# Row stage of a small language-model tower: layer norms, transposes and expert gates in other operations

## The reference

```python
h = tok_ref(x, token_W, pe)
h = h + attn_ref(layernorm(h), ...)       # softmax(qk + bias) * scale @ v, proj, then layernorm(out) * ln2_g + ln2_b
h = h + ffn_ref(layernorm(h), ...)

# ffn_ref
gate_logits = x_flat @ Wg + bg + bias
topk_vals, topk_idx = top_k(gate_logits, 2)
topk_w = softmax(topk_vals, axis=-1)
combine = (one_hot(topk_idx, 8) * topk_w[..., None]).sum(axis=1)
hidden = relu(einsum('td,edh->teh', x_flat, W1) + b1)
out = einsum('ted,te->td', einsum('teh,ehd->ted', hidden, W2) + b2, combine)
```

## Time and profile before

| what | value |
|---|---|
| median of three runs | 143.33 us |
| span of the profiled execution | 143.1 us, 2799 instructions |
| TensorE busy | 106.9 us (75%) |
| VectorE busy | 113.6 us (79%) |
| ScalarE busy | 59.4 us (42%) |
| GpSimd busy | 71.6 us (50%) |
| mean granted TensorE clock | 0.81 of full speed |

### The profile page before, as it was taken

The page is one execution under the profiler, slowest core; times in us unless marked ns, Lnnn a source line. Parts: engine busy times, 40 slices in busy tenths (PEclk is TensorE's granted clock), DMA queues, the critical chain, the costliest instruction groups (busy, mean ns, idle before and its releaser), DMA issues.

```text
span 143.1 us, 2799 instructions
## 1 busy us (share of the span) xinstructions
PE 106.9 (75%) x1029; PEld 61.7 (43%) x1029; DVE 113.6 (79%) x339; ACT 59.4 (42%) x114; POOL 71.6 (50%) x85
## 2 busy tenths in 40 slices
PE   0007655999989999999959759759747959729980
PEld 0003343459448547734623433625422446327650
DVE  6599999893955177169999998998999999999623
ACT  3005600210020464369968942647946625620020
POOL 2059991502620286256968993549399830360000
PEclk9999999999755558659999996986997576896555
DMA  3785000000000000000000000001000001004021
GB/s 82 285 321 216 0 0 0 0 5 1 5 0 0 0 0 0 0 2 7 0 0 7 0 0 0 5 5 32 0 5 2 0 8 33 0 0 110 5 73 37
DMA packets 5397, 4.45 MB, mean 31 GB/s; under 512 B 4515, under 2 KB 4743, under 8 KB 5256
## 3 DMA queue, kind: packets, MB, share of 16 engines
q1 hardware_dynamic: 5162, 4.18, 9.0%
q10 hardware_dynamic: 222, 0.10, 0.4%
HBM read 3.21 MB, written 1.06 MB: 30 GB/s over the span
## 4 chain that ended last, share of the span: by engine, by line
PE 44%; DVE 43%; issue 5%; DMA 3%; ACT 2%; POOL 1%; SPq 0%; DVEq 0%; ACTq 0%; POOLq 0%
PE bank L909 9%; DVE acc L818 6%; PE bank L1060 5%; PE bank L1080 4%; DVE prod L811 4%; PE bank L991 3%; DMA vec<-in_vecs_dram 3%; PE bank L988 3%; DVE xs L777 3%; PE bank L1075 2%; PE bank L1085 2%; DVE oneh_j L639 2%; DVE xs L776 2%; DVE xn L614 2%; PE bank L998 2%
## 5 line engine op out<-in xcount | busy, mean ns | idle before, releaser
L314 POOL TENSOR_TENSOR hid_lo<-hid,hid_hi 128x512 f16<-128x512 f32 (+1 forms) x38 | 41.9, 1118 | 17.3 <-ACT hid_hi L543 17.2
L543 ACT ACTIVATE hid<-bank,b_col 128x512 f32<-128x512 f32 (+1 forms) x40 | 25.8, 648 | 20.4 <-PE bank L1060 20.3
L543 ACT ACTIVATE hid_hi<-bank,b_col 128x512 f16<-128x512 f32 (+1 forms) x38 | 24.5, 645 | 0.0
L818 DVE TENSOR_REDUCE acc<-prod 128x64 f32<-128x512 f32 x18 | 18.6, 1034 | 0.4
L1060 PE MATMUL bank<-xT,w_hi 128*128 128x512 f16 (+1 forms) x40 | 17.3, 432 | 0.6 <-ACT hid_hi L543 0.6
L1060 PE MATMUL bank<-xT,w_lo 128*128 128x512 f16 (+1 forms) x40 | 17.5, 437 | 0.0
L811 DVE TENSOR_TENSOR prod<-bank,comb 128x512 f32<-128x512 f32 x18 | 12.4, 688 | 4.7 <-PE bank L1085 4.3
L442 POOL TENSOR_TENSOR rs<-var,neghalf 128x4 f32<-128x4 f32 (+1 forms) x5 | 4.8, 952 | 20.7 <-DVE var L755 20.6
L1080 PE MATMUL bank<-w_hi,hid_hi 128*128 128x64 f16 x144 | 13.3, 210 | 1.9 <-DVE hid_lo L314 1.9
L1080 PEld LDWEIGHTS bank<-w_hi,hid_hi 128*128 128x128 f16 x144 | 10.9, 108 | 7.4 <-issue 5.2
L1080 PE MATMUL bank<-w_lo,hid_hi 128*128 128x64 f16 x144 | 13.3, 210 | 0.0
(11 more groups left out here) (218 smaller groups left out, 228.1 us busy)
## 6 DMA issues: line engine op xcount, KB each, us to landing
ids_all<-ids_scratch SPq DMA_DIRECT2D x1, 1024.0 KB, 4.7
w_sb<-in_w1g_dram SPq DMA_DIRECT2D x1, 516.0 KB, 5.6
hankel<-in_bias_table_dram SPq DMA_DIRECT2D x1, 512.0 KB, 4.5
out_dram<-looked SPq DMA_DIRECT2D x2, 256.0 KB
table_all<-in_bias_table_dram SPq DMA_DIRECT2D x1, 511.5 KB, 5.0
out_dram<-fin_all SPq DMA_DIRECT2D x3, 128.0 KB
w_sb<-in_w2b_dram SPq DMA_DIRECT2D x1, 260.0 KB, 5.4
vec<-in_vecs_dram SPq DMA_DIRECT2D x1, 200.5 KB, 4.1
```

The source lines that it names most:

```text
L314: return eng.tensor_tensor(hid_lo[:, k % 2, e, 0:m], hid[:, n % HSLOTS, 0:m], hid_hi[:, k % 2, e, 0:m], ALU.subtract)
L543: ins = act.activation(dst, bank[n % 2][:, 0:m], ACT.Relu, bias=b1_col[:, e:e + 1], scale=HSCALE / (XSCALE * XSCALE))
L818: link(dve.tensor_reduce(acc[:, i, :], prod[:, n % 2].rearrange("p e d -> p d e"), AX.X, ALU.add))
```

## The change

The 65th value column becomes the root of 64 times epsilon instead of one, and ScalarE's squares are scaled by 1/64 in total (by 64 to the power -0.5 before squaring), so that one VectorE sum over 65 columns is the variance with its epsilon. Normalising and weighting with ln2_g become one operation for each block, and so do centring and scaling, which writes each row twice, side by side, in f32. The transposes move f32 instead of f16. ScalarE reads the transposed rows from bank 5 with a scale of 64 into f16; then a new VectorE step `low_x` replaces the lower 64 partitions of xT (64 to 127) by the difference between the value in the bank and the f16 just written; `gate` and `first_layer` wait for that one. The gates are made with tanh of half the difference, for both choices at once, and the indices are compared as integers, ahead of the wait for ScalarE. The lists of ScalarE and TensorE keep their order; VectorE's has a `low_x` for each unit. Of the diff, the declarations of tiles and semaphores and ScalarE's list, where only `choice_exp` becomes `choice_tanh`, are left out.

```diff
@@ -42,6 +42,7 @@
 SKIP_ID = 128
 EXPERTS, HID = 8, 128
 EPS = 1e-5
+ROOT = (D * EPS) ** 0.5
 ABSENT = -1e30
 ESCALE = 32768.0
 XSCALE = 64.0
...
@@ -386,7 +380,7 @@
             pool.iota(iota_p[:], [[0, 1]], base=0, channel_multiplier=1,
                       allow_small_or_imprecise_dtypes=True).then_inc(s_const, 1)
             pool.memset(neghalf[:], -0.5)
-            pool.memset(vp[:], 1.0)
+            pool.memset(vp[:], ROOT)
             pool.memset(ones_h[:], 1.0)
             pool.memset(ones_b[:], 1.0).then_inc(s_const, 1)
             pool.wait_ge(s_const, 2)
@@ -514,7 +508,7 @@
                 if g >= 1:
                     act.wait_ge(s_var1, g)
                 act.activation(usq[:, 0:SIZE[g], :], bank[3][:, 0:SIZE[g] * (D + 1)].rearrange("p (b d) -> p b d", d=D + 1),
-                               ACT.Square).then_inc(s_usq, 1)
+                               ACT.Square, scale=D ** -0.5).then_inc(s_usq, 1)
 
             def score_tile(t):
                 act.wait_ge(s_a, t + 1)
@@ -526,7 +520,8 @@
                 act.wait_ge(s_xT, g + 1)
                 if g >= 2:
                     act.wait_ge(s_z, EXPERTS * (g - 1))
-                act.copy(xT[:, g % 2, 0:P * SIZE[g]], bank5h[:, 0:P * SIZE[g]]).then_inc(s_xTsb, 1)
+                act.activation(xT[:, g % 2, 0:P * SIZE[g]], bank[5][:, 0:P * SIZE[g]], ACT.Copy,
+                               scale=XSCALE).then_inc(s_xThi, 1)
 
             def hidden(k, e):
                 n = EXPERTS * k + e
@@ -544,9 +539,9 @@
                                          scale=HSCALE / (XSCALE * XSCALE))
                 ins.then_inc(s_hid, 1)
 
-            def choice_exp(g):
+            def choice_tanh(g):
                 act.wait_ge(s_gd, g + 1)
-                act.activation(ge[:, 0:SIZE[g]], gd[:, 0:SIZE[g]], ACT.Exp).then_inc(s_ge, 1)
+                act.activation(gt[:, 0:SIZE[g]], gd[:, 0:SIZE[g]], ACT.Tanh, scale=0.5).then_inc(s_ge, 1)
 
             def read_look(n):
...
@@ -750,31 +745,43 @@
             def rows_a(g):
                 m = SIZE[g]
                 dve.wait_ge(s_usq, g + 1)
-                dve.tensor_scalar(deps[:, 0:m], usq[:, 0:m, D], EPS, None, ALU.mult)
-                link(dve.tensor_reduce(uss[:, 0:m], usq[:, 0:m, 0:D], AX.X, ALU.add))
-                dve.scalar_tensor_tensor(var1[:, 0:m], uss[:, 0:m], 1.0 / D, deps[:, 0:m], ALU.mult, ALU.add).then_inc(s_var1, 1)
+                dve.tensor_reduce(var1[:, 0:m], usq[:, 0:m], AX.X, ALU.add).then_inc(s_var1, 1)
 
             def rows_b(g):
                 m, u, h, hg = parts_of(g)
                 dve.wait_ge(s_rs1, g + 1)
-                link(rescale(on[:, 0:m], u[:, :, 0:D], rs1[:, 0:m], m))
-                link(dve.tensor_tensor(og[:, 0:m], on[:, 0:m], bcast(vec[:, C_G2:C_G2 + D], [P, m, D], 1), ALU.mult))
+                for i in range(m):
+                    ins = dve.scalar_tensor_tensor(og[:, i, :], u[:, i, 0:D], rs1[:, i:i + 1], vec[:, C_G2:C_G2 + D],
+                                                   ALU.mult, ALU.mult)
+                link(ins)
                 dve.tensor_tensor(hg, og[:, 0:m], h, ALU.add).then_inc(s_h2, 1)
 
             def rows_b2(g):
                 m, u, h, hg = parts_of(g)
                 dve.wait_ge(s_h2, g + 1)
-                row_stats(hg, stat, mv[:, 0:m], var2[:, 0:m], m, 1.0 / (XSCALE * XSCALE), EPS / (XSCALE * XSCALE), s_var2)
-                link(centre(xc[:, 0:m], hg, mv[:, 0:m], m))
+                for i in range(m):
+                    ins = dve.bn_stats(stat[:, i, :], hg[:, i, :])
+                link(ins)
+                for i in range(m):
+                    ins = dve.bn_aggr(mv[:, i, :], stat[:, i, :])
+                link(ins)
+                dve.tensor_scalar(var2[:, 0:m], mv[:, 0:m, 1], EPS, None, ALU.add).then_inc(s_var2, 1)
 
             def rows_c(g):
-                m = SIZE[g]
+                m, u, h, hg = parts_of(g)
                 dve.wait_ge(s_rs2, g + 1)
-                link(rescale(xn[:, 0:m], xc[:, 0:m], rs2[:, 0:m], m))
-                if g >= 2:
-                    dve.wait_ge(s_xT, g - 1)
-                link(dve.tensor_copy(xs[:, g % 2, 0:m, 0, :], xn[:, 0:m]))
-                dve.tensor_tensor(xs[:, g % 2, 0:m, 1, :], xn[:, 0:m], xs[:, g % 2, 0:m, 0, :], ALU.subtract).then_inc(s_xs, 1)
+                if g >= 1:
+                    dve.wait_ge(s_xT, g)
+                for i in range(m):
+                    ins = dve.tensor_scalar(xn[:, i, :, :], bcast(hg[:, i, :], [P, 2, D], 1), mv[:, i, 0:1], rs2[:, i:i + 1],
+                                            ALU.subtract, ALU.mult)
+                ins.then_inc(s_xn, 1)
+
+            def low_x(g):
+                dve.wait_ge(s_xThi, g + 1)
+                half, cols = slice(D, P), slice(0, P * SIZE[g])
+                dve.scalar_tensor_tensor(xT[half, g % 2, cols], bank[5][half, cols], XSCALE, xT[half, g % 2, cols],
+                                         ALU.mult, ALU.subtract).then_inc(s_xTsb, 1)
 
             def choose_a(g):
                 m = SIZE[g]
@@ -786,24 +793,21 @@
                 for i in range(m):
                     ins = dve.max(top[:, i, :], lg[:, i, :])
                 link(ins)
-                dve.tensor_tensor(gd[:, 0:m], top[:, 0:m, 1], top[:, 0:m, 0], ALU.subtract).then_inc(s_gd, 1)
+                dve.tensor_tensor(gd[:, 0:m], top[:, 0:m, 0:2], top[:, 0:m, 1::-1], ALU.subtract).then_inc(s_gd, 1)
                 for i in range(m):
                     ins = dve.max_index(tix[:, i, :], top[:, i, :], lg[:, i, :])
                 link(ins)
-                dve.tensor_copy(tixf[:, :, 0:m], tix[:, 0:m, 0:2].rearrange("p b j -> p j b"))
 
             def choose_b(g):
                 m = SIZE[g]
+                four = [P, m, 2, EXPERTS]
+                sm = sel[:, 0:m]
+                dve.tensor_tensor(sm, iota_row[:, 0:EXPERTS].unsqueeze(1).unsqueeze(1).to_broadcast(four),
+                                  tix[:, 0:m, 0:2].unsqueeze(3).to_broadcast(four), ALU.is_equal)
                 dve.wait_ge(s_ge, g + 1)
-                link(dve.tensor_scalar(gs[:, 0:m], ge[:, 0:m], 1.0, YSCALE, ALU.add, ALU.mult))
-                link(dve.reciprocal(gw[:, 0, 0:m], gs[:, 0:m]))
-                dve.tensor_tensor(gw[:, 1, 0:m], gw[:, 0, 0:m], ge[:, 0:m], ALU.mult)
-                four = [P, 2, m, EXPERTS]
-                sm = sel[:, :, 0:m]
-                link(dve.tensor_tensor(sm, iota_row[:, 0:EXPERTS].unsqueeze(1).unsqueeze(1).to_broadcast(four),
-                                       tixf[:, :, 0:m].unsqueeze(3).to_broadcast(four), ALU.is_equal))
-                link(dve.tensor_tensor(sm, sm, gw[:, :, 0:m].unsqueeze(3).to_broadcast(four), ALU.mult))
-                link(dve.tensor_tensor(comb[:, g % 2, 0:m], sel[:, 0, 0:m], sel[:, 1, 0:m], ALU.add))
+                link(dve.tensor_scalar(gw[:, 0:m], gt[:, 0:m], 1.0, 0.5 / YSCALE, ALU.add, ALU.mult))
+                link(dve.tensor_tensor(sm, sm, gw[:, 0:m].unsqueeze(3).to_broadcast(four), ALU.mult))
+                link(dve.tensor_tensor(comb[:, g % 2, 0:m], sel[:, 0:m, 0], sel[:, 0:m, 1], ALU.add))
 
             def weigh(n):
                 u, i = unit_of(n)
@@ -845,12 +849,12 @@
             one_hot_rows(); late_one_hots(); toeplitz(); toeplitz_flat(); read_k(); read_counts()
             penalties(); early_one_hots(); values(); flat_weights(); row_maxima(); skip_columns()
             bias_parts(); split_exps(); rows_a(0); rows_b(0); rows_b2(0); skip_key(); rows_c(0)
-            key_part(0); skip_key_rows(); choose_a(0); choose_b(0); rows_a(1); rows_b(1); rows_b2(1)
-            key_part(1); rows_c(1); rows_a(2); choose_a(1); rows_b(2); rows_b2(2); weigh(0); key_part(2)
-            gather(0); rows_c(2); weigh(1); choose_b(1); rows_a(3); choose_a(2); gather(1); rows_b(3)
+            key_part(0); skip_key_rows(); low_x(0); choose_a(0); choose_b(0); rows_a(1); rows_b(1); rows_b2(1)
+            key_part(1); rows_c(1); rows_a(2); low_x(1); choose_a(1); rows_b(2); rows_b2(2); weigh(0); key_part(2)
+            gather(0); rows_c(2); weigh(1); choose_b(1); low_x(2); rows_a(3); choose_a(2); gather(1); rows_b(3)
             rows_b2(3); weigh(2); gather(2); weigh(3); choose_b(2); gather(3); weigh(4); key_part(3)
-            gather(4); weigh(5); rows_c(3); gather(5); rows_a(4); choose_a(3); weigh(6); gather(6)
-            rows_b(4); rows_b2(4); weigh(7); gather(7); rows_c(4); weigh(8); gather(8); weigh(9)
+            gather(4); weigh(5); rows_c(3); gather(5); rows_a(4); low_x(3); choose_a(3); weigh(6); gather(6)
+            rows_b(4); rows_b2(4); weigh(7); gather(7); rows_c(4); weigh(8); gather(8); low_x(4); weigh(9)
             choose_b(3); choose_a(4); gather(9); weigh(10); gather(10); weigh(11); gather(11); weigh(12)
             gather(12); weigh(13); choose_b(4); low(4, 3); low(4, 5); gather(13); weigh(14); gather(14)
             weigh(15); gather(15); weigh(16); gather(16); weigh(17); gather(17)
@@ -1025,7 +1029,7 @@
```

(36 more changed lines are left out.)

## The result

The changed kernel takes 148.11 us (median of four runs, 146.7 to 148.68) against 142.79 us before; the ratio is 1.038, with a 95% interval of 1.027 to 1.049. Forecast were 141.1 us and at most 145.8: wrong in sign and outside the range. The four kinds of saving are there, but most of VectorE's is given back in one place, which was rival C.

A forecast was written before the change was run, and what follows sets the result against it. TensorE was taken to bound 43 to 62 us, VectorE 62 to 84. 143.1 + 2.5 - 7.9 + 0.6 + 0.5 + 2.1 = 140.9 us of span, 141.1 us as median, range 138.2 to 145.8.

The forecast's parts named there:

- rival C: Each of four centre-and-scale instructions waits for its own GpSimd subtraction, 2.5 us a unit in three units: 148.6 us; chance 0.12.
- I charge one wait a group, 0.5 us: VectorE's four centre-and-scale instructions per unit wait for GpSimd once, 0.5 us; bounds none and four waits of up to 0.84.
- The gain on VectorE: Removed groups less added ones leave 2.5 us a unit; 7.9 us gained in all, mostly in units 2 to 4.
- The transposes: On TensorE, four f32 transposes cost 0.64 us more at the high clock; 1.28 in unit 1 at the low one.
- The opening of VectorE's stage: VectorE's stage opens 2.5 us late: 1.2 from unit 0's turn to gate, 1.3 from unit 1's transposes.
- The two waits of unit 2: VectorE waits 0.6 us at key_part(2) for late Toeplitz sums, and 0.5 us around low_x(2) and the gate.
- From span to time: Median run time taken as 0.2 us above the span, turning 140.9 us into 141.1.
- Unit 3's stall: low_x(3) behind rows_a(4) and ScalarE's squares delays the gate; 2.1 us more idle before weigh(6).
- Tanh: ScalarE's gates by tanh cost nothing; exp and tanh in one set would mean no table load.
- rival D: TensorE keeps the low clock of 43 to 62 us for part of the next stretch: 145 us; chance 0.12.

The follow-up runs named there:

- e2: Changed kernel with centring as one operation after the variance and scaling as one operation instead of four small ones; 145.3 us, ratio 0.996 to the kernel before.
- e3: Changed kernel with the old second norm and turn, keeping epsilon column, fused weighting, integer compare and tanh gates; 139.61 us, ratio 0.969 to the kernel before.
- e4: Changed kernel with both the single scaling operation (e2) and low_x(3) ahead of rows_a(4) (e1); 141.24 us, ratio 0.971 to the kernel before.
- e7: e4 plus second_layer(6) moved ahead of gate(3) in TensorE's list; 141.61 us against 144.15 before, too scattered for a ratio.
- e9: e3 plus second_layer(6) moved ahead of gate(3) in TensorE's list; 140.27 us against 144.21 before, too scattered for a ratio.
- e5: Changed kernel with GpSimd's subtractions cut to 16 columns, leaving most low halves out of the result; 136.91 us, ratio 0.962 to the kernel before.
- e1: Changed kernel with low_x(3) ahead of rows_a(4) in VectorE's list; 148.26 us, ratio 1.021 to the kernel before.
- e6: Kernel before with GpSimd's subtractions cut to 16 columns, leaving most low halves out of the result; 137.56 us, ratio 0.969 to the uncut kernel before.
- c1: The changed kernel run again unaltered, on the chip of e5 to e7; 147.51 us, ratio 1.032 to the kernel before.
- e10: Changed kernel with the four centre-and-scale instructions as scalar_tensor_tensor with a second SBUF operand; 148.16 us, ratio 1.029 to the kernel before.

## Why the prediction was wrong, step by step

**The step that failed: "I charge one wait a group, 0.5 us".** The four centre-and-scale instructions of a unit paid up to four waits. The charge rested on one pair, var and xc. GpSimd in order of time beside it:

```profile
81.49 1.15 POOL L314 TENSOR_TENSOR hid_lo<-hid,hid_hi 128x512 f16<-128x512 f32 x1
...
82.60 1.41 POOL L314 TENSOR_TENSOR hid_lo<-hid,hid_hi 128x512 f16<-128x512 f32 x1
```

xc started at 82.58, 0.02 us before GpSimd's next subtraction at 82.60, and that one then lasted 1.41 us for 1.15: GpSimd waited for xc. In unit 2 of the changed kernel GpSimd's next started at 71.84 and the second xn at 71.88: 0.04 us later, and VectorE waited. Both were a matter of who came first.

The pair was no accident: in unit 2 of the kernel before, too, var was held (0.37 us), xc ran in 0.41 us from 66.65, and GpSimd's next, from 66.71, lasted 1.37 us; e2, e3, e4, e7 and e9 show the same in unit 2. Behind the 4-column var VectorE's next instruction comes 0.02 to 0.06 us ahead of GpSimd's; behind a 128-column xn it comes 0.04 us too late. That the columns make this difference is read from the start times; no run varies them alone.

The trace of before held the counter-example in a plain form, xn, cast and difference of unit 2, three separate instructions of 0.3 to 0.4 us that took 3.41 us, one of GpSimd's each:

```profile
69.43 1.02 DVE L614 TENSOR_TENSOR xn<-xc,rs 128x256 f32<-128x256 f32 x1
70.48 1.14 DVE L776 CAST xs<-xn 128x256 f16<-128x256 f32 x1
71.65 1.26 DVE L777 TENSOR_TENSOR xs<-xn,xs 128x256 f16<-128x256 f32 x1
```

I had put the waits in the price of what was removed and left the same price out of what was added. Rival C had the mechanism, at 0.12; its price of 2.5 us a unit was 2.5 in unit 4, 3.0 in unit 2 and 0.6 in unit 3, where GpSimd had less in its queue: only the third of the four waited there.

In all the three groups took 6.1 us more than charged. Some 0.7 us of that is no wait: four undisturbed ones take 1.11 us (e5), not 0.88. For the stage from the logits of unit 1 to weigh(13) the sum had 7.9 us of gain less 0.6, 0.5 and 2.1 of delays, 4.7 us net; it became a loss of 1.3 us, 6.0 us worse. That this is so near 6.1, and 140.9 + 6.1 = 147.0 so near the span of 146.3, is partly luck, since the smaller errors told below partly cancel.

The section of the Trainium skill that was cited (SBUF — State Buffer, Who interferes with whom) has the right rule, exclusive, for the whole instruction, for whoever starts first; the traces of GpSimd's subtractions agree, down to the 1.41 us of the other order. Its power operation is different here: beside rsqrt2(3) of the kernel before (85.08, 1.00 us) VectorE's gw<-gw,ge at 85.85 and sel<-iota_row,tixf at 85.93, each with two inputs in SBUF, kept 0.16 and 0.22 us. The measurement decides: not every instruction of GpSimd's holds VectorE up.

**The gain on VectorE.** og, xc, the casts, reciprocal and gw are gone as counted, and what replaced them outside xn costs as priced. In e3 the kept part gives 3.1%. The 7.9 us came only less those 6.1 us.

**The transposes: mis-sized by more than two.** TensorE in order of time, units 1 and 2:

```profile
61.12 1.06 PE L1040 MATMUL bank<-ident,xn 128*128 128x128 f32 x4
61.97 0.63 PE L913 MATMUL bank<-toe_hi,oneh_j 128*128 128x512 f16 x1
62.40 0.63 PE L913 MATMUL bank<-toe_lo,oneh_j 128*128 128x512 f16 x1
...
75.36 0.66 PE L1040 MATMUL bank<-ident,xn 128*128 128x128 f32 x4 [2.13 <-DVE xn L776]
75.85 0.50 PE L1063 MATMUL bank<-xT,w_hi 128*128 128x512 f16 x1
```

In unit 1, beside matmuls of 512 columns that start 0.43 us apart, the four take 0.85 us to the next start, where f16 took 0.42: 0.43 us more, not 1.28. In unit 2 they take 0.49 for 0.23: 0.26 more, not the 0.64 of the high clock. I had doubled the 0.21 us of the prologue's f32 transposes for the low clock, but the 512-column matmuls just ahead of those start 0.43 us apart as well (28.37 and 28.80 us), in a stretch whose granted clock reads 1.00: the price was the low one already.

**The opening of VectorE's stage.** Forecast 2.5 us late, measured 2.1, of which 0.9 come from the prologue, which the change does not touch; the change itself costs 1.2 us, and that the total looks right is luck. Turn and gate of unit 0 cost 0.7 us instead of 1.2, since transposes and low_x (0.43 us) are cheaper.

**The two waits of unit 2, 0.6 and 0.5 us.** They did not come about. key_part(2) starts at 69.17 without a wait, low_x(2) waits 0.16 us and the logits behind it not at all, since VectorE, held up by GpSimd, comes to them late. Instead weigh(2) waited 1.14 us for TensorE.

**From span to time.** The forecast took 0.2 us between the span (143.1) and the median (143.33). These are two executions; in one and the same, time is 1.7 to 1.9 us above the span. The difference to the kernel before, 2.2 us of gain, is not touched by this.

**Unit 3's stall: right in its order, in its size partly by luck.** ScalarE, then VectorE, in order of time:

```profile
95.88 0.60 ACT L523 ACTIVATE xT<-bank 128x512 f16<-128x512 f32 x1 [2.36 <-PE bank L1040]
96.37 0.38 ACT L510 ACTIVATE usq<-bank 128x260 f32<-128x260 f32 x1
```

```profile
93.19 1.94 DVE L776 TENSOR_SCALAR xn<-h_all,mv,rs 128x128 f32<-128x128 f32 x4
...
96.79 0.42 DVE L748 TENSOR_REDUCE var<-usq 128x4 f32<-128x260 f32 x1 [0.26 <-ACT usq L510]
97.24 0.69 DVE L783 SCALAR_TENSOR_TENSOR xT<-bank,xT 64x512 f16<-64x512 f32 x1
98.41 0.19 DVE L789 SCALAR_TENSOR_TENSOR lg<-bank,gb_sum 128x32 f32<-128x32 f32 x1 [0.47 <-PE bank L1047]
...
102.13 0.69 DVE L815 TENSOR_TENSOR prod<-bank,comb 128x512 f32<-128x512 f32 x1 [2.37 <-PE bank L1088]
```

Read, squares, sum, low_x, logits come one after the other as forecast, and weigh(6) starts 7.0 us after xn's end instead of 4.8: 2.2 us, forecast 2.1. Only 1.7 of them lie ahead of the gate (it starts 2.9 us after xn's end instead of 1.1, forecast 3.2); the rest lies behind it, where the same work took 4.1 us instead of 3.7 at a granted clock of 0.50 instead of 0.59. e1 confirms the place; e7 and e9 show no gain in the total from taking the stall away.

**Tanh: right.** ScalarE's list holds one table load, as before:

```profile
1.85 1.28 ACT L474 ACT_TABLE_LOAD   x1 [1.85 <-issue]
```

This agrees with the Trainium skill (ScalarE: Activation LUTs, Table sets), by which exp and tanh lie in one set.

**The clock, rival D.** 62 to 84 us went from 0.94 to 0.76, and weigh(2) waited 1.14 us for TensorE where VectorE had been last. It may be part of the loss, of a size that no run isolates; e5 and e6 show that without the waits for GpSimd the kernels are level, with clocks near each other (0.845 and 0.857 over the span).

## What to carry over

Price a VectorE instruction from SBUF to SBUF by what GpSimd runs at that time, and price added instructions as the removed ones were: beside GpSimd's subtractions back to back each of the four cost one of them (here 1.1 us), however short it is. One 512-column operation (0.69 to 1.3 us) then beat four of 128 (1.9 to 4.4 us), so a fusion is judged by how many such instructions it leaves, not by their columns. The other side pays too: where VectorE came first, GpSimd's subtraction took 1.4 to 1.6 us. Read the pace of TensorE off a matmul of known size next to the row that gives a price.

## What was not expected

The prologue, whose instructions here are the same, varies from kernel to kernel. VectorE in order of time, before and then after:

```profile
16.20 1.25 DVE L661 SCALAR_TENSOR_TENSOR toe_lo<-hankel,toe_hi 128x1024 f16<-128x1024 f32 x1
17.48 0.36 DVE L665 COPY toe_hi<-toe_hi 128x384 f16<-128x384 f16 x1
17.76 1.21 DVE L666 COPY toe_lo<-toe_lo 128x384 f16<-128x384 f16 x1
```

```profile
16.38 2.12 DVE L656 SCALAR_TENSOR_TENSOR toe_lo<-hankel,toe_hi 128x1024 f16<-128x1024 f32 x1
18.53 1.08 DVE L660 COPY toe_hi<-toe_hi 128x384 f16<-128x384 f16 x1
19.53 2.30 DVE L661 COPY toe_lo<-toe_lo 128x384 f16<-128x384 f16 x1
```

The three take 2.8 us in one and 5.5 in the other, and GpSimd's weight preparation lies beside them in another order: its b_col scaling takes 1.16 us before, 0.60 after, and its cast to w_hi 1.04 before, 1.91 after (part is made up soon after: +0.9 us at rows_a(0)). c1, e7, e9 and e10 show the long form as well; e1 has the short form and is 1.9 us ahead of the changed kernel at rows_a(0), with the same list up to there. A microsecond or two of any comparison here is this draw, and it repeats from run to run of one kernel: c1, run later and apart, has it too.
